# A bidirectional state-space block: whole-tile activations of ScalarE moved ahead of its V build inside each scan unit

## The reference

```python
h = layernorm(x) * (1 + ca) + sa
x = x + ga * (layernorm2(mamba1(ln1(h)) + flip(mamba2(flip(ln1(h))))) + ln1(h))
h = layernorm(x) * (1 + cb) + sb
x = x + gb * ffn(h)
```

```python
h = exp(dt * A) * h + (dt * xt) * B_t
y = sum over the states of h * C_t
```

## Time and profile before

| what | value |
|---|---|
| median of 3 executions | 12675.65 us |
| their range | 12661.51 to 12689.12 us |
| the profiled execution, own time | 12639.29 us |
| its span in the profile | 12637.5 us |
| DVE busy | 11838.3 us (94%) |
| POOL busy | 11415.9 us (90%) |
| ACT busy | 10856.0 us (86%) |
| PE busy | 10215.3 us (81%) |
| mean granted clock of PE | 0.901 |

### The profile page before, as it was taken

The page is one execution under the profiler, slowest core; times in us unless marked ns, Lnnn a source line. Parts: engine busy times, 40 slices in busy tenths (PEclk is TensorE's granted clock), DMA queues, the critical chain, the costliest instruction groups (busy, mean ns, idle before and its releaser), DMA issues.

```text
span 12637.5 us, 179504 instructions
## 1 busy us (share of the span) xinstructions
PE 10215.3 (81%) x51484; PEld 5829.8 (46%) x51484; DVE 11838.3 (94%) x7032; ACT 10856.0 (86%) x23460; POOL 11415.9 (90%) x5972
## 2 busy tenths in 40 slices
PE   5678878888787887878878888887878878788887
PEld 2334544445444444544445444454544445444445
DVE  5999999999999999999999999999999999999992
ACT  5888988898888998988989888898889989888882
POOL 4999999999999999999999999999999999999992
PEclk7778989999898998989989898998989989889898
DMA  2223333333333333333333333333333333333332
GB/s 85 84 86 115 123 111 129 124 109 115 115 129 116 118 126 105 131 114 123 122 115 116 113 127 123 109 123 108 130 113 120 123 112 129 111 126 123 108 111 97
DMA packets 610252, 1458.92 MB, mean 115 GB/s; under 512 B 68928, under 2 KB 110032, under 8 KB 604672
## 3 DMA queue, kind: packets, MB, share of 16 engines
q1 hardware_dynamic: 609152, 1446.18, 35.2%
HBM read 1355.09 MB, written 90.83 MB: 114 GB/s over the span
## 4 chain that ended last, share of the span: by engine, by line
issue 27%; PE 21%; ACT 17%; POOL 16%; DVE 15%; DMA 1%; DVEq 0%; POOLq 0%; SPq 0%; ACTq 0%
POOL state L1298 13%; DVE state L1268 10%; ACT state L1082 6%; ACT v_sb L1095 5%; PE driven L882 5%; PE q_ps L837 4%; DVE driven L1257 3%; PE y_ps L904 3%; PE q_ps L824 2%; PE p_ps L745 1%; PE p_ps L753 1%; POOL v_sb L1376 1%; PE b_ps L872 1%; ACT L1082 1%; PE p_ps L769 1%
## 5 line engine op out<-in xcount | busy, mean ns | idle before, releaser
L1298 POOL TENSOR_TENSOR state<-state,c_rep 128x1024 f32<-128x1024 f32 x4096 | 9660.7, 2390 | 773.3 <-DVE state L1268 767.6
L1268 DVE TENSOR_TENSOR_SCAN state<-state,driven 128x1024 f32<-128x1024 f32 x4096 | 9093.4, 2269 | 260.7 <-PE driven L882 252.0
L1082 ACT ACTIVATE state<-ud_rep,cols_sb 128x512 f32<-128x512 f32 x8192 | 5212.3, 710 | 6.6 <-PE y_ps L904 4.1
L1095 ACT ACTIVATE v_sb<-u_t,b_t 128x128 f32<-128x128 f32 x12288 | 4062.3, 505 | 940.0 <-PE driven L882 936.6
L882 PE MATMUL driven<-consts_sb,v_sb 128*128 128x128 f32 x16384 | 2631.8, 313 | 1284.8 <-DVE state L1268 1260.5
L882 PEld LDWEIGHTS driven<-consts_sb,v_sb 128*128 128x128 f32 x16384 | 2130.5, 161 | 2445.0 <-DVE state L1268 1745.6
L904 PE MATMUL y_ps<-state,consts_sb 128*32 128x512 f32 x16384 | 2420.8, 668 | 568.8 <-POOL state L1298 567.9
L1257 DVE TENSOR_TENSOR driven<-ud_rep,b_ps 128x1024 f32<-128x1024 f32 x2048 | 2389.7, 1212 | 18.1 <-DMA ud_rep<-ud_rows 18.1
L837 PE MATMUL q_ps<-hid,wq_sb 128*128 128x256 f32 x7936 | 2049.5, 403 | 144.7 <-ACT hid L1060 76.0
L837 PEld LDWEIGHTS q_ps<-hid,wq_sb 128*128 128x128 f32 x7936 | 1478.9, 196 | 1012.9 <-issue 821.4
L1376 POOL TENSOR_TENSOR v_sb<-u_t,b_t 128x512 f32<-128x512 f32 x1024 | 1070.3, 1045 | 36.5 <-issue 23.6
(11 more groups left out here) (141 smaller groups left out, 5533.5 us busy)
## 6 DMA issues: line engine op xcount, KB each, us to landing
c_rep<-bc_rows SPq DMA_DIRECT2D x2048, 256.0 KB, 3.0
ud_rep<-ud_rows SPq DMA_DIRECT2D x512, 512.0 KB, 4.2
wq_sb<-in_h SPq DMA_DIRECT2D x512, 512.0 KB, 3.9
wq_sb<-in_f SPq DMA_DIRECT2D x128, 512.0 KB, 4.0
wp_sb<-in_win SPq DMA_DIRECT2D x64, 512.0 KB, 4.5
dt_sb<-conv_taps SPq DMA_DIRECT2D x32, 1024.0 KB, 5.5
ud_rows<-u_pad SPq DMA_DIRECT2D x128, 256.0 KB, 3.3
ud_rows<-dt_sb SPq DMA_DIRECT2D x128, 256.0 KB, 3.5
```

What stands on the lines that cost most here:

```text
L1082: ins = act.activation(state[:, unit % STATE_RING, j, :], ud_rep[:, nth % 2, j, 1, :], ACT.Exp, scale=a_neg[:, d, c, j, g:g + 1])
L1095: ins = act.activation(v_sb[:, unit // 2 % V_RING, tt, :, :, n].rearrange("p j e -> p (j e)"), u_t[:, nth % 2, tt, :], ACT.Identity, scale ...
L1268: dve.tensor_tensor_scan(flat, flat, driven[:, q % DRIVE_RING].rearrange("p j t -> p (j t)"), 0.0, ALU.mult, ALU.add).then_inc(scanned, 1)
L1298: pool.tensor_tensor(part, part, c_rep[:, unit % ROW_RING, :].unsqueeze(1).to_broadcast([P, 2, T]), ALU.mult).then_inc(was_read, 1)
```

## The change

A function `own_work` names ACT's side steps that read no result of PE directly: `xc`, `exp`, `one`, `ln`, `sz`, the normalisations, and the SiLU and GELU of the hidden layer. In a unit ACT now works `decays`, then these, then `make_v`, then the copies. `ACT_SIDE` is sorted in the same way, so that the counts of the semaphore follow the order of work. No instruction is added or removed, and all other engines keep their streams. The line numbers of the changed kernel are larger by 5 from there on, up to the last part of the diff.

```diff
@@ -95,6 +95,11 @@
     return [(s + 2, part, name + "_rstd", 9)] + scaled, [(s + 3, part, name + "_norm", TT)], dve
+
+
+def own_work(name):
+
+    return name in ("xc", "exp", "one", "ln", "sz") or name.endswith("norm") or name[:4] in ("silu", "gelu")
@@ -147,7 +152,7 @@
-    act.sort(key=lambda x: x[1:3] not in from_q)
+    act.sort(key=lambda x: (not own_work(x[2]), x[1:3] not in from_q))
@@ -948,9 +953,9 @@
-            def side(at, unit):
+            def side(at, unit, own):
                 for s, part, name, _ in ACT_SIDE:
-                    if s == unit and at.has(part):
+                    if s == unit and at.has(part) and own_work(name) == own:
                         step(at, part, name)
@@ -1103,19 +1108,17 @@
             def body(at):
                 for unit in range(UNITS):
+                    if in_scan(at, unit + 2):
+                        decays(at, unit + 2, 0)
+                        decays(at, unit + 2, 1)
+                    side(at, unit, True)
                     if unit % 2 == 0:
-                        if in_scan(at, unit + 2):
-                            decays(at, unit + 2, 0)
-                            decays(at, unit + 2, 1)
                         if in_scan(at, unit + V_AHEAD):
                             make_v(at, unit + V_AHEAD, 0)
                     else:
-                        if in_scan(at, unit + 2):
-                            decays(at, unit + 2, 0)
-                            decays(at, unit + 2, 1)
                         if in_scan(at, unit + V_AHEAD - 1):
                             make_v(at, unit + V_AHEAD - 1, 1)
-                    side(at, unit)
+                    side(at, unit, False)
```

## The result

The changed kernel takes 12696.4 us in the median of 14 executions (12685.46 to 12719.21), the kernel before, measured beside it, 12660.1 us (14 executions, 12634.94 to 12695.67). The ratio is 1.003, with an interval of [1.0023, 1.0038]: slower. The forecast was 12632 us and faster. The profiled execution of the changed kernel took 12697.74 us, 1.84 of them outside its span of 12695.9 us; the two profiled spans lie 58.4 us apart.

The account below looks back on a forecast made before the run. DVE, busy 94% of the span, was taken as the bound, so only its idle time could be won. Gains of 85 us less losses of 28 and 13 gave -44 us: 12675.65 - 44 = 12632 us, range 12590 to 12705.

Parts of the forecast that it names:

- scans of units 57 and 125: Waits of 1.55 and 2.05 us vanish because PE gets unit 54's GELU and unit 122's GELU 2.56 us earlier.
- `dt`, unit 110: `ln` comes 1.3 us earlier, so `dt` starts without a wait, ahead of POOL's multiplication; gain 2.23 us in 14 rounds.
- `rest`, unit 108: `one` comes 2.56 us earlier, but a longer second part takes back 2.05 of 2.61 us; gain 0, bounds 0 and 0.56.
- late copy at unit 97: Unit 94's network copy ends 3.2 us later, making PE's chain and unit 97's scan 1.9 us late; 28 us in 15 rounds.
- the clock behind it: PE at half clock in unit 95 costs 1.8 us, taken in half of the rounds: 15 x 0.9 = 13 us.
- unit 29: Unit 26's late copy delays PE 2.0 us, hidden by DVE's 2.11 us wait for B's eviction; otherwise 2 us a round.
- the whole chain to unit 97 at half clock: Upper bound of the clock loss: low clock from unit 95 to the transposes; with lateness, 1.9 + 5.6 = 7.5 us.
- The slower rival: PE at half clock from the late copies in units 95 and 27 to the transposes; 12773 us, chance 0.17.
- its own mark, 5.7 us a round: Loss in a round from which half clock behind the late copies decides for slower: 85 / 15 = 5.7 us.
- The second rival: The clock falls at both late copies every round; units 97 and 29 lose 81 us together; 12672 us, chance 0.26.
- ACT's idle time can't be filled: ACT's 936.6 us idle ahead of the V build stays or grows, as units with own work show no such wait.
- The prediction's own sign of being wrong: Wrong if `rest` returns its whole 2.6 us, unit 97 shows over 4 us, or the mean clock falls below 0.901.

Follow-up runs that it names:

- short 95: Changed kernel plus three 128x512 matmuls on PE, results unread, in its wait ahead of unit 95's side steps; 12673.21 us, ratio 1.0016 to the kernel before.
- PE kept busy: Changed kernel plus unread 128x512 matmuls on PE, four ahead of unit 123's side steps and four behind unit 125; 12667.27 us, ratio 1.0004 to the kernel before.
- `xc` alone: Kernel before, with only `xc` moved ahead of the V build; 12762.12 us, ratio 1.0094 to the kernel before.
- softplus alone: Kernel before, with only `exp`, `one` and `ln` moved ahead of the V build; 12634.13 us, ratio 0.999 to the kernel before.
- hidden layer alone: Kernel before, with only the hidden layer's SiLU and GELU moved ahead of the V build; 12651.17 us, ratio 1.0004 to the kernel before.

## Why the prediction was wrong

Term by term, in us a round; what was forecast, and what the runs showed:

| term | forecast | measured |
|---|---|---|
| scans of units 57 and 125 | -3.6 | -1.43 and -1.91 |
| `dt`, unit 110 | -2.23 | -2.32 |
| `rest`, unit 108 | 0 (down to -0.56) | -0.23 |
| late copy at unit 97 | +1.9 | +1.80 (short 95) |
| the clock behind it | +0.9 | +1.91 (change less short 95) |
| unit 29 | 0 (up to +2) | +0.59 |
| units 58 to 60 | none | +0.86 |
| units 114 to 117 | none | +1.37 |
| end of the round | none | +1.90 |
| small places | none | +1.21 |

**The gains were right**, to 0.3 us each, and the step that a switch costs ACT 1.30 us as well: the rows of unit 94 have the load at 5338.81 and `xc` at 5340.10, 1.29 us in all.

**The step that failed first is the clock, "I take it in half of the rounds: 15 x 0.9 = 13 us".** By the lengths of unit 96 the clock fell in 11 of 14 rounds (granted 0.50 to 0.58 over the eight matmuls behind the late copy, 1.00 in the other 3), and in 7 of them, like the fifth, it stayed low into the B projection (0.59 to 0.62, and 3.03 to 3.17 us for it instead of 1.88), so the term was 1.9 us, not 0.9. That the bounds of the prediction took this in ("the whole chain to unit 97 at half clock") is right, but the half was a guess between two rows that differed, and it was the wrong end of it. The lateness itself, 1.9 us, was right to 0.1.

**Unit 29, "Hidden: nothing, if that cover stays".** The cover was used up: DVE's wait of 2.11 us for the eviction of B has gone, the scan waits 3.03 us for PE instead, and 0.59 us more than the cover are left.

**What decided the sign is a term that the prediction put at nothing, without a reason.** Each gain was worked out in its own unit and carried to the end of the round as won; what PE's clock does in units that lose no copy was not asked. Units 58 to 60, 114 to 117, the small places and the end of the round take 5.3 us a round in the profiled execution, nearly all that was gained there.

- Units 58 to 60: the rows show how the time is lost. ACT has no idle time there, and PE, earlier, waits for the next copy instead; it comes in the 12 rounds in which PE's matmuls behind the GELU are slow (granted clock 0.53 or 0.54), and why they are slow in these is open.
- The end of the round: the path of the loss is shown. PE runs at low clock (granted 0.50 to 0.59 in the 4 us from the first scan of unit 127 in the 13 rounds that branch back, 1.00 in the kernel before), the network's last matmuls end too late to let DVE branch back under cover, and with PE kept busy 1.80 of the 1.90 us are back. Why the clock falls is open; the wait ahead of it grew from 1.71 to 2.18 us in the seventh round, but `xc` alone and softplus alone lose there after shorter ones.
- Units 114 to 117: the loss goes with the clock. In 9 of the 14 rounds the mean granted clock is 0.50 to 0.57 from 14 to 6 us ahead of the first scan of unit 115, and unit 114 lasts 6.0 to 6.4 us; in the other 5 it is 1.00, and unit 114 lasts 4.37 us as before. Why it falls stays open: the loss came with `xc` alone and with the SiLU and GELU alone, was not there with everything but `xc`, and went with the six long matmuls at unit 95 but not with three. No run was made for it.

**The rivals.** The measured time, 12696 us, lies inside the stated range, but not by the forecast's sum: it got there through these losses, and that is luck. The slower rival had the right kind of mechanism, PE at half clock (granted 0.50) behind the late copies. But its own mark, 5.7 us a round from the two places, was not reached: they lose 3.71 and 0.59. The second rival, gain and loss cancel through the clock, is nearest in its sum at these two places, 5.4 us forecast against 4.3. Both looked only at the places where a copy comes later. That ACT's idle time can't be filled was right: 921.7 us of 936.6 are still there. The prediction's own sign of being wrong, a mean clock below 0.901, came true with 0.890.

## What to carry to other kernels

When an engine in the middle has no idle time, moving its steps about moves waits about: price the step that comes later by what the consumer's clock does after the wait, not by the lateness alone (in unit 96 the clock cost 1.9 us, the lateness 1.8), and follow a step that comes earlier to the next thing that its consumer waits for. A reorder of many kinds of steps is best tried kind by kind: here one of them, `xc`, cost more than all others won, and leaving it where it was made a version 0.4% faster than the kernel before. Look at the end of a loop on the engine that bounds the time: here the next scan came 3.0 us after the branch back in both kernels; it waited 0.35 us where 2.33 us of work stood queued ahead of the last instruction that has to wait, and 2.40 us where none did.

## What was not expected of the hardware

- The same wait of 2.98 us on PE was followed by eight matmuls at a granted clock of 1.00 in 3 rounds (1.99 us), at 0.50 in 7 (3.78 us) and at 0.54 to 0.58 on average in 4 (3.38 to 3.60 us). With 2.84 us of other matmuls in it, unit 96 had its length of full clock, 7.4 to 7.5 us, in all 14.
- From DVE's branch instruction at the end of the loop to the next scan it took 3.0 to 3.4 us in the 13 rounds that branch back; behind the last round of the loop it took 0.5 in the run with the hidden layer alone. The list of waits puts it down to another engine (ACT's decays), and only the chain shows it.
- A matmul of 512 columns between these float32 tiles (`ident` and `cols_sb`) appears as two instructions and took 0.9 us at a granted clock of 1.00, twice the 0.47 that was expected of it.
